# The second layer by sorted (token, expert) pairs in 44 steps, where every token ran all eight experts

## The chip, the cores and the metric

One core of a Trainium2 chip runs the whole kernel. The metric is the device time of one execution in microseconds, lower is better. Engines are named as the profile names them: PE (matrix multiply), DVE (vector), ACT (scalar), POOL (GpSimd), SP (issues transfers).

## What is computed

`x` is 2048 tokens of 512 numbers. Two layers follow each other, each with a layer norm ahead of it and a residual around it.

```python
x = x + xattn(layernorm(x), itok, ctx, ctx, ctx)
x = x + ffn(layernorm(x), G, gate_w, up_w, down_w, lora_A, lora_B)
# xattn, for a token whose id lies in quarter e of the vocabulary (4 of them):
#   h = x @ ctx[e].T ;  y = (silu(h) * h) @ ctx[e].T          512 x 512 both
# ffn: 8 experts, each 512 -> 64 (gate and up) -> 512, and LoRA 512 -> 16 -> 512
#   w = softmax(x @ G), all but the two highest set to 0
#   out = sum_e w_e * (down_e(silu(gate_e x) * up_e x) + lora_B_e(lora_A_e x))
```

Only two of the eight weights `w_e` of a token are not zero.

## The kernel before

**Layer one.** A prologue sorts the tokens by their quarter into 19 tiles of 128 tokens (`STEPS`), of which each has one matrix. Step k gathers tile k (POOL, `gather`), normalises it, transposes it on PE (`turn_x`, 4 blocks of 128x128), multiplies by the matrix (`l1_first`, 12 matmuls of 512 columns: each operand is split in a high part on ACT and a low part on DVE, and three of the four products of parts are taken), applies silu and the product on ACT and DVE, transposes again (`turn_act`), multiplies again (`l1_second`, 12 matmuls of 512 columns), adds the residual (DVE, `residual`), and POOL stores the rows to DRAM (`x1_rows`) at their compact places.

**Layer two.** It takes the 16 full tiles of 2048 rows in order. All eight experts are computed densely for each tile: `l2_first` makes 12 matmuls in each of three column groups (392, 384 and 384 columns: gate, up and LoRA of all experts and the 8 router logits), `l2_gates` makes the routing weights in twelve small DVE operations, `l2_act` multiplies them in, with zeros for the six experts not chosen, and `l2_second` makes 15 matmuls of 512 columns.

**Order.** Each engine executes its own list in program order. A semaphore wait holds up everything behind it on that engine. The order in a step is written by hand. In layer one PE does `turn_act(k-1)`, `l1_first(k)`, `turn_x(k+1)`, `l1_second(k-1)`, and DVE does `lo_act(k-1)`, `residual(k-2)`, `statistics(k+3)` with `normalise(k+2)` inside it, `l1_gate(k)`, `lo_x(k+1)`. A semaphore is waited for and the instruction after it is the one that the profile shows waiting. The layer-norm statistics of layer two's rows are made by the same `statistics` when the stored tile is read back by SP (L223).

## Time and profile before

| what | us |
|---|---|
| median of 3 runs | 333.06 |
| lowest and highest of them | 330.94, 333.4 |
| the profiled execution | 331.94 |
| its span, first to last instruction | 330.1 |
| layer one, from its third step's `turn_act` to layer two's first | 33.63 to 146.03 |
| layer two, to the last store's issue | 146.03 to 322.54 |
| PE busy | 304.6 |
| DVE, POOL, ACT busy | 212.8, 108.7, 82.9 |

The profiled execution's own time has 1.84 us outside of its span. Positions in the table are microseconds from the start of the span.

### The profile page before, as it was taken

To read this page: it belongs to the slowest core of one execution; us is meant where nothing else is said; L and a number is where in the kernel's file an instruction comes from. 1 tells how busy PE (TensorE), PEld (TensorE's weight loads), DVE (VectorE), ACT (ScalarE), POOL (GpSimd) and SP (SyncE) were. 2 spreads that over 40 slices of the span, in tenths; PEclk is the share of its full clock that TensorE was granted. 3 is DMA by queue.
4 is the path that set the end of the run, shared out by engine and by line. 5 is a ranking of instruction groups with operands and counts; after the bars stand their busy time and mean duration, and the time that the engine had idled before them with its cause. 6 is when DMAs were issued, how large, how long until landed. Compare 5 with 4: busy or idle time off the path is not lost.

```text
span 330.1 us, 5390 instructions
## 1 busy us (share of the span) xinstructions
PE 304.6 (92%) x1636; PEld 269.1 (82%) x1637; DVE 212.8 (64%) x603; ACT 82.9 (25%) x158; POOL 108.7 (33%) x118
## 2 busy tenths in 40 slices
PE   1649997999999999999999999999999999999990
PEld 1636885888888888889999999999999999999970
DVE  7879865674666576467865686658756776557520
ACT  3523213232332323231212211221212121212110
POOL 1779834566566445431120111101110111011111
PEclk9979999999999999999999999999999999999996
DMA  7462685122212323222210122011110000000000
GB/s 252 164 213 73 165 318 213 70 95 71 90 64 95 95 64 115 75 64 65 66 64 0 64 64 64 14 50 64 64 38 26 32 32 32 0 32 34 32 28 37
DMA packets 8074, 26.37 MB, mean 80 GB/s; under 512 B 1408, under 2 KB 1408, under 8 KB 7424
## 3 DMA queue, kind: packets, MB, share of 16 engines
q0 software_dynamic: 4320, 14.16, 12.5%
q1 hardware_dynamic: 3744, 12.08, 11.3%
q8 instruction: 5, 0.08, 0.1%
q14 instruction: 5, 0.04, 0.0%
HBM read 17.06 MB, written 9.18 MB: 79 GB/s over the span
## 4 chain that ended last, share of the span: by engine, by line
PE 81%; POOL 6%; DMA 6%; issue 2%; DVE 2%; ACT 0%; DVEq 0%; ACTq 0%; POOLq 0%
PE p_y L681 10%; PE p_y L686 10%; PE p_y L682 10%; PE p_h L681 7%; PE p_h L686 7%; PE p_h L682 7%; PE p_aT L676 5%; PE p_xT L670 4%; PE p_a L682 3%; PE p_a L681 3%; PE p_a L686 3%; PE p_b L682 3%; PE p_b L686 3%; PE p_b L681 3%; DMA xin<-x,gather_row 3%
## 5 line engine op out<-in xcount | busy, mean ns | idle before, releaser
L492 DVE TENSOR_TENSOR aT_lo<-p_aT,aT_hi 128x512 fp32r<-128x512 f32 (+1 forms) x35 | 26.3, 752 | 85.8 <-ACT aT_hi L320 83.1
L253 POOL DMA_INDIRECT out<-xout,out_row x16 | 16.6, 1035 | 134.8 <-DVE xout L500 133.1
L320 ACT ACTIVATE aT_hi<-p_aT 128x512 fp32r<-128x512 f32 (+1 forms) x35 | 22.7, 648 | 106.2 <-PE p_aT L676 100.1
L253 POOL DMA_INDIRECT x_rows<-xout,x_row x19 | 19.7, 1038 | 55.0 <-DVE xout L500 54.7
L681 PE MATMUL p_y<-ctx_hi,aT_hi 128*128 x76 | 31.4, 414 | 2.5 <-DVE xout L500 2.4
L681 PE MATMUL p_y<-w_hi,aT_hi 128*128 128x512 f32 x75 | 30.7, 410 | 0.0
L682 PE MATMUL p_y<-ctx_lo,aT_hi 128*128 x76 | 29.8, 392 | 0.0
L681 PE MATMUL p_h<-ctx_hi,xT_hi 128*128 x72 | 29.8, 413 | 0.0
L682 PE MATMUL p_y<-w_lo,aT_hi 128*128 128x512 f32 x75 | 29.4, 393 | 0.0
L682 PE MATMUL p_h<-ctx_lo,xT_hi 128*128 x72 | 28.3, 392 | 0.0
L247 POOL TENSOR_TENSOR rstd<-var_eps,neg_half 128x1 f32<-128x1 f32 x35 | 23.1, 659 | 13.0 <-DVE var_eps L475 12.9
L469 DVE BATCH_NORM_STATS2 bn<-xin 128x6 f32 (+1 forms) x35 | 24.0, 684 | 2.5 <-DMA xin<-x,gather_row 2.5
L670 PE MATMUL p_xT<-ident,xn 128*128 128x128 f32 x140 | 21.1, 273 | 3.6 <-DVE xn L483 3.6
L488 DVE TENSOR_TENSOR xT_lo<-p_xT,xT_hi 128x512 fp32r<-128x512 f32 x35 | 23.9, 684 | 0.7 <-PE p_a L686 0.6
L483 DVE TENSOR_SCALAR xn<-xin,mean_var,rstd 128x512 f32 (+1 forms) x35 | 21.5, 616 | 4.3 <-DVE bn L469 3.5
L316 ACT ACTIVATE xT_hi<-p_xT 128x512 fp32r<-128x512 f32 x35 | 20.9, 596 | 9.8 <-PE p_xT L670 9.8
L670 PEld LDWEIGHTS p_xT<-ident,xn 128*128 128x128 f32 x140 | 17.3, 141 | 7.1 <-issue 3.4
L500 DVE TENSOR_TENSOR xout<-p_y,xin 128x512 f32<-128x512 f32 x34 | 23.1, 681 | 0.0
L681 PE MATMUL p_a<-w_hi,xT_hi 128*128 128x392 f32 x64 | 23.1, 361 | 0.0
L676 PEld LDWEIGHTS p_aT<-ident,act 128*128 128x128 f32 x156 | 19.2, 141 | 4.5
L676 PE MATMUL p_aT<-ident,act 128*128 128x128 f32 x156 | 22.8, 273 | 0.0
L682 PE MATMUL p_a<-w_lo,xT_hi 128*128 128x392 f32 x64 | 21.9, 342 | 0.0
(145 smaller groups left out, 663.5 us busy)
## 6 DMA issues: line engine op xcount, KB each, us to landing
whole<-ctx_t SPq DMA_DIRECT2D x4, 1024.0 KB, 6.5
xin<-x_rows SPq DMA_DIRECT2D x16, 256.0 KB, 2.6
whole<-w_up SPq DMA_DIRECT2D x4, 580.0 KB, 5.1
whole<-w_down SPq DMA_DIRECT2D x1, 1280.0 KB, 8.0
xin<-x,gather_row POOLq DMA_INDIRECT x19, 3.4
x_rows<-xout,x_row POOLq DMA_INDIRECT x19, 3.1
out<-xout,out_row POOLq DMA_INDIRECT x16, 2.9
ids<-token_ids SPq DMA_DIRECT2D x1, 8.0 KB, 1.6
```

Source lines behind the costliest of these rows:

```text
L247: nc.gpsimd.tensor_tensor(rstd[:, r % 2:r % 2 + 1], var_eps[:, r % 2:r % 2 + 1], neg_half[:], ALU.pow).then_inc(rstd_ready, 1)
L253: nc.gpsimd.indirect_dma_start(out=to, out_offset=bass.IndirectOffsetOnAxis(ap=rows, axis=0), in_=xout[:, r % 2, :], in_offset=None).then_ ...
L320: nc.scalar.activation(aT_hi[:, 0:cols], p_aT[:, 0:cols], ACT.Copy).then_inc(ahi_ready, 1)
L469: nc.vector.bn_stats(bn6[:, parity, :], x_rows_of(r)).then_inc(bn6_ready, 1)
L488: nc.vector.tensor_tensor(xT_lo[:], p_xT[:], xT_hi[:].bitcast(F32), ALU.subtract).then_inc(xlo_ready, 1)
L492: nc.vector.tensor_tensor(aT_lo[:, 0:cols], p_aT[:, 0:cols], aT_hi[:, 0:cols].bitcast(F32), ALU.subtract).then_inc(alo_ready, 1)
L500: nc.vector.tensor_tensor(xout[:, parity, :], y[:], x_rows_of(r), ALU.add).then_inc(xout_ready, 1)
L670: last = nc.tensor.transpose(p_xT[:, blk(i)], xn[:, parity, blk(i)], ident[:])
L676: last = nc.tensor.transpose(p_aT[:, blk(i)], act[:, blk(i)], ident[:])
L681: nc.tensor.matmul(to, hi[:, blk(i)], w_hi(i), start=(i == 0), stop=False)
L682: nc.tensor.matmul(to, hi[:, blk(i)], w_lo(i), start=False, stop=False)
L686: last = nc.tensor.matmul(to, lo[:, blk(i)], w_hi(i), start=False, stop=(i == blocks - 1))
```

## The change

The prologue sorts once instead of twice. Layer one has the same 19 steps, but each step now also prepares layer two for its own tile, which stays in SBUF (`rec`, 8 tiles): `residual` is followed by a second `bn_stats`, `statistics2` ends the statistics, ACT subtracts the mean (`centre`), PE transposes the tile (`turn_x2`), ACT copies it (`copy_x2T`), PE multiplies it by the router matrix in fp32 (`route`, 4 matmuls of 8 columns), and DVE takes the two highest experts (`choose`). After each batch of four tiles `owners` and `places` on DVE and `rank` on PE work out the routing weights and the place of each (token, expert) pair, in a list sorted by expert. POOL scatters each tile's rows twice (`scatter`), to `rows_a` under the token's lower expert and to `rows_b` under the higher one.

Layer two has 44 steps (`PAIRS`), 22 for the lower experts and 22 for the higher ones (phases A and B). Step s loads 128 sorted rows of one expert (SP, `load_pair`, an address that is read from SBUF), transposes them (`tx`), multiplies by that expert's 144 columns (`up`: 12 accumulating matmuls of 144 columns), applies the gate (`gate_silu`, `gate_up`), transposes the 80 columns (`ta`), multiplies back (`down`, 3 matmuls of 512 columns), and adds (`pair_finish`). Phase A scatters its sums by rows to `sums_b`; phase B loads those (`load_sum`) and scatters to `out`. Iteration i of each engine's list holds parts of several steps (`pair_iteration`): PE does up(i), ta(i-1), down(i-2), tx(i+2).

The instructions are no longer in loops: they are all written out. The core of the diff:

```diff
+NB = E2 - 1
+CAP = TOKENS + P
+DUMMY = NB * CAP
+XROWS = DUMMY + P
+META = 4
+ROW = D + META
+REC = D + 2 * META
+RSTD, MEAN, GATE, DEST = range(META)
+NOWHERE = 1 << 20
+EARLY = 7
+PHASE = TILES + NB - 1
...
+            def load_pair(s):
+                if s >= ARING:
+                    sp.wait_ge(stored[(s - ARING) % ORING], 16 * ((s - ARING) // ORING + 1))
+                row = sp.value_load(pair_row[0:1, s:s + 1], min_val=0, max_val=DUMMY)
+                rows = rows_a if s < PHASE else rows_b
...
+            def load_sum(s):
+                n = s - PHASE
+                if n >= YRING:
+                    sp.wait_ge(pair_done, s - YRING + 1)
+                row = sp.value_load(pair_row[0:1, s:s + 1], min_val=0, max_val=DUMMY)
+                sp.dma_start(pair_sum[:, n % YRING, :], sums_b[bass.ds(row, P), :]).then_inc(sum_landed[n % YRING], 16)
...
+            for i in range(RRING):
+                sp.wait_ge(scattered_a[i], 16 * (BATCHES[EARLY_BATCH][1] // RRING))
+            for s in range(ARING):
+                load_pair(s)
+            sp.wait_ge(lists_ready, 2)
+            for e in range(NB):
+                fill_region(0, e)
...
+            for s in range(EARLY, PAIRS + 3):
+                if s == PHASE:
+                    for t in range(STEPS - RRING, STEPS):
...
+                    for i in range(ORING):
+                        sp.wait_ge(stored[i], 16 * ((PHASE - i + ORING - 1) // ORING))
+                if s - 3 >= PHASE:
+                    load_sum(s - 3)
+                if EARLY + 2 <= s < EARLY + 2 + NB:
...
+            def scatter(t, phase):
+                b = t // 4
+                pool.wait_ge(dest_ready, b + 1)
+                pool.wait_ge(stats_put, b + 1)
+                rows, cols, done = ((rows_a, slice(0, ROW), scattered_a), (rows_b, slice(META, REC), scattered_b))[phase]
                 nc.gpsimd.indirect_dma_start(
-                    out=to, out_offset=bass.IndirectOffsetOnAxis(ap=rows, axis=0), in_=xout[:, r % 2, :],
...
+            def store(s):
+                pool.wait_ge(pair_done, s + 1)
...
+            def centre(t):
+                sc.wait_ge(stats2_ready, t + 1)
+                nc.scalar.activation(record(t), record(t), ACT.Identity, bias=neg_mean2[:, t:t + 1]).then_inc(xc_ready, 1)
...
+            def pair_iteration(i):
+                if 0 <= i - 1 < PAIRS:
+                    ah2(i - 1)
+                if i < PAIRS:
+                    gate_silu(i)
+                if i + 2 < PAIRS:
+                    hi2(i + 2)
+                if i < PHASE:
+                    mean_back(i)
...
+            for k in range(STEPS):
+                if k >= 1:
+                    hi_act(k - 1)
+                if k >= 2:
+                    centre(k - 2)
...
+            def residual(t):
+                dve.wait_ge(y_ready, t + 1)
+                if t >= RRING:
+                    dve.wait_ge(scattered_a[t % RRING], 16 * (t // RRING))
+                    dve.wait_ge(scattered_b[t % RRING], 16 * (t // RRING))
+                nc.vector.tensor_tensor(record(t), p_y[:], xin[:, t % XRING, :], ALU.add).then_inc(x1_ready, 1)
+                dve.wait_ge(x1_ready, t + 1)
+                nc.vector.bn_stats(bn6_2[:, t % 2, :], record(t)).then_inc(bn6_2_ready, 1)
+            def statistics2(t):
+                dve.wait_ge(bn6_2_ready, t + 1)
+                nc.vector.bn_aggr(mean_var2[:, t, :], bn6_2[:, t % 2, :]).then_inc(mean2_ready, 1)
+                dve.wait_ge(mean2_ready, t + 1)
+                nc.vector.tensor_scalar(neg_mean2[:, t:t + 1], mean_var2[:, t, 0:1], -1.0, None, ALU.mult)
+                nc.vector.tensor_scalar(var_eps2[:, t:t + 1], mean_var2[:, t, 1:2], EPS, None,
...
+            def pair_finish(s):
+                if s >= ORING:
+                    dve.wait_ge(stored[s % ORING], 16 * (s // ORING))
+                dve.wait_ge(o_ready, s + 1)
+                if s < PHASE:
+                    dve.wait_ge(x1_back, s + 1)
+                    other = x1_pair[:, s % 2, :]
+                else:
+                    n = s - PHASE
+                    dve.wait_ge(sum_landed[n % YRING], 16 * (n // YRING + 1))
+                    other = pair_sum[:, n % YRING, :]
+                nc.vector.scalar_tensor_tensor(pair_out[:, s % ORING, :], p_o[s % 2][:], pair_meta(s, GATE), other,
+                                               ALU.mult, ALU.add).then_inc(pair_done, 1)
...
+            for k in range(STEPS):
+                if k >= 1:
+                    lo_act(k - 1)
+                if k >= 2:
+                    residual(k - 2)
+                if k + 3 < STEPS:
+                    statistics(k + 3, between=k + 2)
+                elif k + 2 < STEPS:
+                    normalise(k + 2)
+                if k >= 2:
+                    statistics2(k - 2)
+                if k >= 3:
+                    choose(k - 3)
+                    if (k - 3) % 4 == 3:
+                        owners((k - 3) // 4)
...
+            def turn_x2(t):
+                pe.wait_ge(xc_ready, t + 1)
+                if t >= 1:
+                    pe.wait_ge(x2T_out, t)
...
+            def route(t):
+                c = t % 2 * E2
+                pe.wait_ge(x2T_out, t + 1)
...
-            def l2_first(r):
-                pe.wait_ge(xhi_ready, r + 1)
-                for to, c0, c1, ready in ((p_a, 0, GATE_B0, part_a_ready), (p_b, GATE_B0, GATE_C0, part_b_ready),
-                                          (p_h, GATE_C0, UPW, part_c_ready)):
-                    w = up_part(c0, c1)
-                    hi_passes(to[:, 0:c1 - c0], xT_hi, KB, *w)
-                    pe.wait_ge(xlo_ready, r + 1)
-                    lo_passes(to[:, 0:c1 - c0], xT_lo, KB, w[0]).then_inc(ready, 1)
...
-            def l2_second(r, to=p_y, between=None):
-                if to is p_y:
-                    pe.wait_ge(xout_ready, r)
-                pe.wait_ge(ahi_ready, r + 1)
...
+            def tx(s):
+                pe.wait_ge(pair_landed[s % ARING], 16 * (s // ARING + 1))
...
+                rows = pair_x_of(s)
+                for i in range(KB):
+                    last = nc.tensor.transpose(p_x[s % 2][:, blk(i)], rows[:, blk(i)], ident[:])
+                last.then_inc(tx_ready, 1)
...
+            def up(s):
+                e = pair_matrices(s)
+                to = p_u[s % 2]
+                def w(i, part_of):
+                    return up_w[:, bass.ds(e + i * E2, 1), part_of, :].rearrange("p a f -> p (a f)")
...
+                else:
+                    pe.wait_ge(gated_ready, s - 1)
+                hi_passes(to[:, 0:UP], lambda i: xT_hi[:, s % 2, blk(i)], KB, lambda i: w(i, 0), lambda i: w(i, 1))
+                pe.wait_ge(lo2_ready, s + 1)
+                lo_passes(to[:, 0:UP], lambda i: xT_lo[:, s % 2, blk(i)], KB, lambda i: w(i, 0)).then_inc(u_ready, 1)
...
+            def down(s):
+                e = pair_matrices(s)
+                cols = slice(s % 2 * P, s % 2 * P + P)
+                w = [down_hi[0:DK, bass.ds(e, 1), :].rearrange("p a f -> p (a f)"),
+                     down_lo[0:DK, bass.ds(e, 1), :].rearrange("p a f -> p (a f)")]
...
+                nc.tensor.matmul(to, aT_hi[0:DK, cols], w[0], start=True, stop=False)
+                nc.tensor.matmul(to, aT_hi[0:DK, cols], w[1], start=False, stop=False)
+                pe.wait_ge(al2_ready, s + 1)
+                nc.tensor.matmul(to, aT_lo[0:DK, cols], w[0], start=False, stop=True).then_inc(o_ready, 1)
+            def pair_iteration(i):
+                if i < PAIRS:
+                    up(i)
+                if 0 <= i - 1 < PAIRS:
+                    ta(i - 1)
+                if 0 <= i - 2 < PAIRS:
+                    down(i - 2)
+                if i + 2 < PAIRS:
+                    tx(i + 2)
             pe.wait_ge(rows_ready, 1)
+            turn_x(0)
...
+            for k in range(STEPS):
+                if k >= 2:
+                    turn_act(k - 1)
+                l1_first(k, between=turn_x1 if k == 0 else (lambda: turn_act(0)) if k == 1 else None)
+                if 1 <= k < STEPS - 1:
+                    turn_x(k + 1)
+                if k >= 2:
+                    turn_x2(k - 2)
+                if k >= 6 and (k - 6) % 4 == 0:
+                    if (k - 6) // 4 == EARLY_BATCH:
+                        total(EARLY_BATCH)
+                    rank((k - 6) // 4)
+                if k >= 1:
                     l1_second(k - 1)
-            turn_act(STEPS - 1, KB)
-            pe.wait_ge(w2_lo_ready, -(-DOWN0 // PIECE))
-            l2_first(STEPS)
-            turn_x(STEPS + 1, (STEPS + 1) % 2)
...
```

What stands on PE in layer one between the first product and the second, ahead of the change (`p_h` is the first product's bank, `p_y` the second's):

```order
L686 MATMUL p_h<-ctx_hi,xT_lo 128x512 [waits xlo_ready]
L686 MATMUL p_h<-ctx_hi,xT_lo 128x512 x3
L670 MATMUL p_xT<-ident,xn 128x128 [waits xn_ready]
L670 MATMUL p_xT<-ident,xn 128x128 x3
L691 TENSOR_LOAD step_expert
L691 ISA x2
L681 ISA [waits ahi_ready,xout_ready]
L681 MATMUL p_y<-ctx_hi,aT_hi 128x512
```

and with it (`rec` is the tile after layer one, two steps back):

```order
L979 MATMUL p_h<-ctx_hi,xT_lo 128x512 [waits xlo_ready]
L979 MATMUL p_h<-ctx_hi,xT_lo 128x512 x3
L910 MATMUL p_xT<-ident,xn 128x128 [waits xn_ready]
L910 MATMUL p_xT<-ident,xn 128x128 x3
L924 MATMUL p_x2T<-ident,rec 128x128 [waits x2T_out,xc_ready]
L924 MATMUL p_x2T<-ident,rec 128x128 x3
L968 TENSOR_LOAD step_expert
L968 ISA x2
L974 ISA [waits ahi_ready,x1_ready]
L974 MATMUL p_y<-ctx_hi,aT_hi 128x512
```

The transposes of `rec` stand ahead of the second product and wait for `xc_ready`, which ACT's `centre` gives.

DVE in the same step, before, from `lo_act` on:

```order
L492 TENSOR_TENSOR aT_lo<-p_aT,aT_hi 128x512 [waits ahi_ready]
L500 TENSOR_TENSOR xout<-p_y,xin 128x512 [waits stored1,y_ready]
L469 BN_STATS bn<-xin 128x6 [waits x1_landed1]
L483 TENSOR_SCALAR xn<-xin,mean_var,rstd 128x512 [waits xT_ready,rstd_ready,bn6_ready]
L473 BN_AGGR mean_var<-bn 128x2
L475 TENSOR_SCALAR var_eps<-mean_var 128x1 [waits mean_ready]
L504 TENSOR_TENSOR act<-silu,p_h 128x512 [waits silu_ready]
L488 TENSOR_TENSOR xT_lo<-p_xT,xT_hi 128x512 [waits xhi_ready]
```

and with the change, behind the same `aT_lo` and the sum, which now is written to `rec`:

```order
L658 BN_STATS bn_2<-rec 128x6 [waits x1_ready]
L620 BN_STATS bn<-xin 128x6 [waits x_landed3]
L634 TENSOR_SCALAR xn<-xin,mean_var,rstd 128x512 [waits xT_ready,rstd_ready,bn6_ready]
L624 BN_AGGR mean_var<-bn 128x2
L626 TENSOR_SCALAR var_eps<-mean_var 128x1 [waits mean_ready]
L662 BN_AGGR mean_var<-bn_2 128x2 [waits bn6_2_ready]
L664 TENSOR_SCALAR neg_mean<-mean_var 128x1 [waits mean2_ready]
L665 TENSOR_SCALAR var_eps<-mean_var 128x1
L671 COPY logits<-p_rt 128x8 [waits logits_ready]
L673 MAX top<-logits 128x8 [waits logits_out]
L674 MAX_INDEX top_at<-top,logits 128x8 [waits route_step]
L649 TENSOR_TENSOR act<-act,p_h 128x512 [waits silu_ready,route_step]
```

Between the sum and the gate (`act<-`) now stand a second `BN_STATS`, three more small operations and the choice of experts (L671 to L674). ACT's `centre` waits for L665.

SP in layer two, before:

```order
L214 DMA whole<-w_down 128x2560
L223 DMA xin<-x_rows 128x512 [waits xout_ready,stored1,stored0] x2
L223 DMA xin<-x_rows 128x512 [waits xout_ready,x1_landed0,stored1,stored0]
L223 DMA xin<-x_rows 128x512 [waits xout_ready,x1_landed1,stored1,stored0]
L223 DMA xin<-x_rows 128x512 [waits xout_ready,x1_landed0,stored1,stored0]
```

and with the change, in phase B:

```order
L271 DMA pair_sum<-sums_b 128x512
L262 TENSOR_LOAD pair_row [waits stored1]
L262 ISA x2
L264 ISA
L264 DMA pair_x<-rows_b 128x516
L270 TENSOR_LOAD pair_row [waits pair_done]
L270 ISA x2
L271 ISA
L271 DMA pair_sum<-sums_b 128x512
```

Each load now waits for the store of six steps before, reads its address from SBUF and alternates with a load of sums.

## Rows read from the trace of the kernel before

**Rows 1.** The page: busy time of each engine, and the chain by engine
```profile
PE 304.6 (92%) x1636; PEld 269.1 (82%) x1637; DVE 212.8 (64%) x603; ACT 82.9 (25%) x158; POOL 108.7 (33%) x118
...
PE 81%; POOL 6%; DMA 6%; issue 2%; DVE 2%; ACT 0%; DVEq 0%; ACTq 0%; POOLq 0%
```

**Rows 2.** Timeline of PE, layer one: start, length (us), engine, line, tiles
```profile
33.63 0.60 PE L676 MATMUL p_aT<-ident,act 128*128 128x128 f32 x4
...
94.72 0.60 PE L676 MATMUL p_aT<-ident,act 128*128 128x128 f32 x4
...
97.93 0.60 PE L670 MATMUL p_xT<-ident,xn 128*128 128x128 f32 x4
98.28 0.48 PE L681 MATMUL p_y<-ctx_hi,aT_hi 128*128 x1
...
101.14 0.60 PE L676 MATMUL p_aT<-ident,act 128*128 128x128 f32 x4
...
146.03 0.60 PE L676 MATMUL p_aT<-ident,act 128*128 128x128 f32 x4
```

**Rows 3.** Timeline of ACT and of DVE in the same step
```profile
95.36 0.60 ACT L320 ACTIVATE aT_hi<-p_aT 128x512 fp32r<-128x512 f32 x1 [2.56 <-PE p_aT L676]
...
95.99 0.69 DVE L492 TENSOR_TENSOR aT_lo<-p_aT,aT_hi 128x512 fp32r<-128x512 f32 x1 [2.11 <-ACT aT_hi L320]
96.60 0.68 DVE L500 TENSOR_TENSOR xout<-p_y,xin 128x512 f32<-128x512 f32 x1
97.19 0.68 DVE L469 BATCH_NORM_STATS2 bn<-xin 128x6 f32 x1
97.92 0.55 DVE L483 TENSOR_SCALAR xn<-xin,mean_var,rstd 128x512 f32 x1
98.38 0.17 DVE L473 BATCH_NORM_AGGREGATE mean_var<-bn 128x2 f32<-128x6 f32 x1
```

**Rows 4.** Timeline of DVE: two small operations, the second waiting for the first
```profile
151.44 0.20 DVE L528 RECIPROCAL z_rest_inv<-z_rest 128x8 f32<-128x8 f32 x1
151.68 0.17 DVE L530 TENSOR_TENSOR z_exp<-z_silu,z_rest_inv 128x8 f32<-128x8 f32 x1
```

**Rows 5.** Timeline of PE, layer two: the act transposes that begin a row
```profile
156.00 0.71 PE L676 MATMUL p_aT<-ident,act 128*128 128x128 f32 x5
...
307.04 0.71 PE L676 MATMUL p_aT<-ident,act 128*128 128x128 f32 x5
```

**Rows 6.** Timeline of PE: short and wide matmuls
```profile
11.70 4.90 PE L662 MATMUL p_y<-below,ones 128*128 128x128 f32 x32
...
232.44 0.34 PE L681 MATMUL p_a<-w_hi,xT_hi 128*128 128x392 f32 x1
232.61 0.34 PE L682 MATMUL p_a<-w_lo,xT_hi 128*128 128x392 f32 x1
```

**Rows 7.** Timeline of PE at its slow and its full clock
```profile
19.85 0.63 PE L670 MATMUL p_xT<-ident,xn 128*128 128x128 f32 x4 [3.25 <-DVE xn L483]
...
22.39 0.63 PE L681 MATMUL p_a<-ctx_hi,xT_hi 128*128 x1
22.82 0.63 PE L682 MATMUL p_a<-ctx_lo,xT_hi 128*128 x1
...
52.66 0.49 PE L681 MATMUL p_y<-ctx_hi,aT_hi 128*128 x1 [2.40 <-DVE xout L500]
...
53.23 0.39 PE L681 MATMUL p_y<-ctx_hi,aT_hi 128*128 x1
```

**Rows 8.** Timeline of POOL in the step of Rows 2
```profile
97.56 1.03 POOL L253 DMA_INDIRECT x_rows<-xout,x_row  x1 [1.77 <-DVE xout L500]
```

**Rows 9.** The page: DMA issues, KB each, us from issue to landing
```profile
xin<-x_rows SPq DMA_DIRECT2D x16, 256.0 KB, 2.6
...
x_rows<-xout,x_row POOLq DMA_INDIRECT x19, 3.1
```

**Rows 10.** Timeline of POOL: the last store
```profile
322.54 0.96 POOL L253 DMA_INDIRECT out<-xout,out_row  x1 [1.77 <-DMA out<-xout,out_row]
```

More of the change, by code:

```diff
@@ L561, in _ @@
+            def pair_iteration(i):
+                if 0 <= i - 1 < PAIRS:
+                    al2(i - 1)
+                if i < PAIRS:
+                    gate_up(i)
+                if 0 <= i - 2 < PAIRS:
+                    pair_finish(i - 2)
+                if i + 2 < PAIRS:
+                    lo2(i + 2)
+            split_ctx(0, 0)
+            split_ctx(1, 0)
+            statistics(0)
+            statistics(1, between=0)
             split_ctx(1, 1)
             lo_x(0)
-            normalise(one(1), first_use=True)
+            normalise(1)
@@ L564, in _ @@
             split_ctx(2, 0)
[L565 removed]
+            statistics(2)
             split_ctx(2, 1)
[L568 to L591 removed]
@@ L628, in _ @@
[L628 to L641 removed]
+            constants()
@@ new lines, in _ @@
+            lo_act(STEPS - 1)
+            residual(STEPS - 2)
+            statistics2(STEPS - 2)
+            choose(STEPS - 3)
+            lo2(0)
+            lo2(1)
+            residual(STEPS - 1)
+            choose(STEPS - 2)
+            statistics2(STEPS - 1)
+            pair_iteration(0)
+            choose(STEPS - 1)
+            owners(len(BATCHES) - 1)
+            pair_iteration(1)
+            places(len(BATCHES) - 1)
+            pair_iteration(2)
+            whole_lists()
+            for i in range(3, PAIRS + 2):
+                pair_iteration(i)
@@ L773, in _ @@
[L773 to L784 removed]
+                turn_x(1)
@@ new lines, in _ @@
+            turn_act(STEPS - 1)
+            turn_x2(STEPS - 2)
+            l1_second(STEPS - 1)
+            route(STEPS - 2)
+            tx(0)
+            tx(1)
+            turn_x2(STEPS - 1)
+            pe.wait_ge(w2_lo_ready, PIECES)
+            pair_iteration(0)
+            route(STEPS - 1)
+            pair_iteration(1)
+            total(len(BATCHES) - 1)
+            rank(len(BATCHES) - 1)
+            pair_iteration(2)
+            for i in range(3, PAIRS + 2):
+                pair_iteration(i)
```

1086 lines of the change are left out of this document (611 added, 475 removed).

## Prediction

> **What bounds the kernel now.** The page first: PE is busy 92% of the span, DVE 64%, and the chain that ended last lies on PE for 81% [rows 1]. So read PE's steps. In layer one the transposes that begin a step start at 94.72 and again at 101.14, 6.42 us apart, with no idle time marked in between [rows 2]; from 33.63 to 146.03 there are 17 such steps. In layer two 14 rows of tiles take from 156.00 to 307.04, 10.79 us each [rows 5]. DVE and ACT have slack: the low part of a step's second operand follows PE's transposes by 1.27 us, while PE has the first product to make [rows 2, 3]. PE sets the pace of both layers, and the last store's issue comes at 322.54, 7.56 us before the span ends [rows 10].
>
> What the change removes is large. Layer two takes 322.54 - 146.03 = 176.5 us, for eight experts of which six get zeros. A step of pairs holds 12 x 144 + 3 x 512 = 3264 columns against 21600 of a row of tiles, so 44 steps have 144 thousand against 346 thousand. The question is what the waits between the engines make of that.
>
> **Layer one with the change.** I take t = 0 at the first `turn_act` transpose of a step and walk the order of each engine. High part on ACT at 0.64, `lo_act` on DVE at 1.27 (95.99 - 94.72), `residual` at 1.88 [rows 2, 3]. The new `bn_stats` of the result must wait for it: an operation of 512 that waits for the one before starts 0.73 behind it (97.19 to 97.92), one that doesn't 0.6 [rows 3]. So it starts at 2.61, the old `bn_stats` at 3.21, `normalise` at 3.94, `bn_aggr` at 4.40 (0.46, rows 3). Then come five small operations, three of them behind a wait at 0.24 each [rows 4], so `stats2_ready` is there at 5.25. ACT's `centre` takes 0.60 as other ACTs of 512 do [rows 3]: 5.85. PE has meanwhile made the first product and `turn_x`, which ends at 3.56 (98.28 - 94.72, rows 2), and now stands at `turn_x2`, whose wait for `centre` stands **ahead of the second product**. It goes on at 5.95, needs 0.35 (97.93 to 98.28), then the second product 2.86 (98.28 to 101.14) [rows 2]: 9.16. Then `route`, 4 fp32 matmuls. The row of 16 fp32 matmuls of 128 columns (32 passes, 4.90 us) gives 0.30 each [rows 6]; 8 columns may cost less, since the weight loads may set this, so 0.9 to 1.2 for four, and I take 1.2, that row. The next step begins at **10.35 us instead of 6.42**. PE has no way round this: `residual` of tile k-2 stands behind `lo_act(k-1)` on DVE, which waits for this step's transposes. The idle part is 5.95 - 3.56 = 2.4 us a step.
>
> Sixteen steps of 10.35 are 165.6. In the steps 6, 10 and 14 `rank` on PE waits some 0.8 more for `owners`. Step 18 has no statistics of a tile to come, but its `rank` waits for the sum over 16 tiles: I count the same small operations to 10.7. The first one-hots are ready earlier, as one sort is left, which gives back 1 us at the start. So `turn_act(18)` starts at 33.63 - 1 + 165.6 + 2.4 + 10.7 = **211.3**, where it was 146.03: +65. What hides beside it: two scatters a tile on POOL (1.03 each, rows 8), with its gather and split some 8 of 10.4 us; `places` on DVE (about 14 small operations, 3 us), which ends before the next `lo_act`; the weight splits on ACT.
>
> **Between the layers.** From 211.3 = A on. DVE has `places` and `early_list` (8 operations on one partition) ahead of `lo_act(18)`, until A+1.3. POOL has `inverse_deviation2(17)` ahead of the last early scatters, which needs `statistics2(17)`, A+3.9. It ends at A+4.5, four scatters at 1.03 follow, and the last lands 3.1 us after its issue at A+7.6 [rows 8, 9]: A+10.7. SP's loads follow: I allow 0.5 for reading the address, then 2.6 to landing [rows 9]: `tx(0)` at A+14. DVE has `lo2(0)` and `lo2(1)` ahead of `residual(18)`, so the last tile's `turn_x2` comes at A+20. Then `up(0)`, `route(18)`, `choose(18)`, `owners(4)`, `rank(4)`, `places(4)` and `whole_lists` follow one another on PE, ACT and DVE with three iterations between them (about 40 small operations, 9 us, the rest PE and ACT): A+42. SP then makes seven loads of a place and seven fills, 0.7 each, and load 7 waits for the last of them to land: A+53, and iteration 5 ends at **A+57**. After such idle stretches the clock costs something: after 3.25 us of idle and four transposes PE's matmuls stood 0.43 us apart (22.39 to 22.82), the lower level of the two (1.2 GHz), where twelve else take 2.86, 0.24 each [rows 7, 2]; some 3 us of this are in the 57.
>
> **The steps of pairs.** A term with no row is the start-to-start time p of a 144-column matmul of split operands. Below: columns alone, 0.17 us for 392 (232.44 to 232.61) [rows 6], 0.065 for 144. Above: fp32 at 128 columns, 0.30 [rows 6], 0.335 for 144. The rows nearest in width are this one and the transposes of 128, four of which take 0.35 to 0.44, 0.11 each [rows 2]; scaled to 144 they are 0.335 and 0.12, and I take the middle, **0.23**, since either could be the kin. PE's own work in an iteration is 12 x 0.23 + 0.11 + 3 x 0.23 + 0.44 = 4.0 us. The other bound is a ring of waits: load s waits until store s-6 has landed. From the start of iteration i: `up` 2.76, an allowance of 0.3 for the address, `ta` 0.11, `down` 0.69, `pair_finish` 0.1 + 0.68, POOL starts 0.28 after the result (96.60 + 0.68 to 97.56), lands 3.1, SP 0.5, load 2.6, `tx` 0.15 + 0.44 [rows 3, 8, 9]: 11.7 us, and this `tx` ends three iterations after it began, so T is at least 3.9. The two are alike; with what they don't share I take T = 4.2. DVE's four operations of a step (0.6, 0.6, and some 0.9 for the small ones) and POOL's 1.03 lie beside it. In phase B three transfers of 256 KB fall in 4.2 us, 190 GB/s, which may add 0.1 to 0.3 and is in the range.
>
> Iterations 6 to 41: 36 x 4.2 = 151. Between the phases `load_sum(22)` waits for the last store of phase A, and load 26 behind it: 7.3 us where 3.7 are there, +3.6. The end: iterations 42 and 43 to the end of `up`, 6.8, the chain through `ta`, `down` and `pair_finish` 3.4, and from the last issue to the end 7.6 as before [rows 10]: 17.8.
>
> **Sum:** 211.3 + 57 + 151 + 3.6 + 17.8 = 440.7 of span, and 1.84 outside of it: **443 us**, against 331.94 of the profiled execution, which lies 1.1 under the median of 333.06. Layer one and what follows it cost 65 + 57, layer two's 176.5 shrink only to 172.
>
> **Rivals.**
> (a) Short matmuls go by columns, p = 0.065. Then `up` takes 0.78, PE's work is 2.0, but the ring of waits still gives 9.76 / 3 = 3.3 us. 36 x 0.9 = 32 less, and 8 + 2 less between the layers and at the end: 401. The 392-column rows speak for it, the fp32 rows against. In the Trainium skill, "TensorE: Matmul & The Clock Gate", section "Back-to-back issue gap", the array takes one column a cycle and narrow matmuls in a stream come about 81 ns apart; the wide rows here agree with a column rule (0.24 us for 512, 0.17 for 392), and by it the time would be this rival's, an estimate; no row here shows it for split operands of 144.
> (b) They go like fp32, p = 0.335: PE's work is 5.3, T = 5.5, 36 x 1.3 = 47 more and 10 more around it: 500.
> (c) The clock falls in layer one too, since PE idles 2.4 us in every step. At 0.43 a matmul the second product takes 2.4 us more, 17 steps, 41: 484. Against it stands the row with 2.40 us of idle ahead of it: the matmul two places behind follows in 0.57 us (52.66 to 53.23), where two take 0.86 at the lower level [rows 7]. The Trainium skill's same page, section "Part 1: The HAM clock gate", has the clock fall after idle time and rise after steady work; both are seen here, at 19.85 to 22.82 [rows 7], but a gap repeated in every step isn't.
> (d) The other side: the round trips don't bind, since the engines run further ahead of one another than I read from their lists, and occupancy alone sets the time. Layer one is then 6.42 + 0.35 + 1.2 = 8.0 a step on PE, 33 + 17 x 8.0 = 169, some 10 between, 44 steps at DVE's 2.4, 106, and 15: 302. It turns faster than before when 110 of the 141 us that I count for waits and slow short matmuls are not there. Nothing in the order of the instructions allows it in layer one.
>
> **How the numbers follow.** The forecast (p from 0.12 to 0.28) has 0.52, 415 to 470; (a) 0.25, 385 to 415; (b) 0.08; (c) 0.08; (d) and other ways to be faster 0.05, equal 0.02. The range 385 to 485 holds the forecast, (a) and (c), 0.85. Under 1% can't be told from no change here: faster 0.05, same 0.02, slower 0.93.
>
> **What would show it.** In the profile after: 10.35 us between `turn_act` groups, with PE idle 2.4 us before the `rec` transposes, released by ACT's `rec`; the first `pair_x` transposes 14 us after the last `turn_act`; the start-to-start time of `up_w` matmuls; T of 4.2 and idle time before `pair_x` transposes released by a DMA. The prediction is wrong if `centre` is not what PE waits for, or if steps of pairs run under 3.3 us.

## The result and the profile after

The changed kernel took **496.12 us** (492.09 to 498.39, 4 runs) against 332.1 for the kernel before on the same chip: a ratio of 1.492, 95% interval 1.480 to 1.504. The direction was as forecast; the time lies 53 us above the forecast and 11 above its range. The profiled execution has a span of 490.3 us, 49.6 more than the predicted 440.7.

The page after, first what answers to [rows 1] (busy times of PE), then PE's busy tenths and the granted clock in tenths, in 40 slices of 12.3 us, then the chain by engine:
```profile
PE 388.8 (79%) x1799; PEld 328.9 (67%) x1799; DVE 237.3 (48%) x713; ACT 135.8 (28%) x301; POOL 155.7 (32%) x172
...
PE   2687777778788787886298099999897999799990
...
PEclk9999889899899989988655555555755555755555
...
PE 55%; DVE 13%; issue 11%; DMA 10%; ACT 5%; SPq 2%; POOL 2%; POOLq 0%; DVEq 0%
```
Read the two rows of digits together. In layer one PE is at 7 or 8 tenths and the clock near full. From the 21st slice on, in the steps of pairs, PE is busy nearly all the time but for some waits, **and the clock is at 5 tenths**, its lower level, in nearly every slice. The view by stretches says it sharper (us, busy time and count of PE, PEld, DVE, ACT and POOL, then PEclk, DMA share, GB/s):
```profile
160.00:215.00 55.00, 43.74 (x231) 34.85 (x228) 31.82 (x108) 18.51 (x39) 22.06 (x25) 0.97 0.16 57
215.00:270.00 55.00, 38.33 (x168) 33.03 (x168) 26.84 (x113) 13.51 (x36) 18.20 (x19) 0.64 0.27 93
...
300.00:350.00 50.00, 49.86 (x220) 44.72 (x219) 22.45 (x55) 18.23 (x44) 10.08 (x11) 0.54 0.46 154
...
353.00:417.00 64.00, 59.61 (x244) 52.57 (x242) 24.90 (x60) 14.71 (x39) 11.18 (x12) 0.50 0.40 118
```

**Layer one** goes as forecast. PE's timeline of a step, beside [rows 2]:
```profile
112.56 0.63 PE L916 MATMUL p_aT<-ident,act 128*128 128x128 f32 x4
...
115.83 0.60 PE L910 MATMUL p_xT<-ident,xn 128*128 128x128 f32 x4
118.49 0.65 PE L924 MATMUL p_x2T<-ident,rec 128*128 128x128 f32 x4 [2.06 <-ACT rec L442]
119.36 0.49 PE L974 MATMUL p_y<-ctx_hi,aT_hi 128*128 x1 [0.22 <-issue]
...
122.26 0.95 PE L936 MATMUL p_rt<-route_w,x2T 128*128 128x8 f32 x8
123.06 0.31 PE L916 MATMUL p_aT<-ident,act 128*128 128x128 f32 x1
```
10.50 us from `turn_act` to `turn_act` (10.35 forecast), PE idle 2.06 us ahead of the `rec` transposes and released by ACT's `centre` (2.4 forecast). The next step, in which `rank` stands between, takes 12.78; the fp16 matmuls of `rank` end, the queue idles again, and the second product falls to the lower clock at its second matmul, after which they start 0.40 to 0.43 us apart:
```profile
128.99 0.66 PE L924 MATMUL p_x2T<-ident,rec 128*128 128x128 f32 x4 [2.07 <-ACT rec L442]
...
130.60 0.50 PE L974 MATMUL p_y<-ctx_hi,aT_hi 128*128 x1 [0.73 <-issue]
130.93 0.60 PE L975 MATMUL p_y<-ctx_lo,aT_hi 128*128 x1
131.33 0.63 PE L974 MATMUL p_y<-ctx_hi,aT_hi 128*128 x1
131.75 0.63 PE L975 MATMUL p_y<-ctx_lo,aT_hi 128*128 x1
```

**The hand-over**, PE: the last `turn_act` of layer one (A), the first pair's transposes, the last tile's, and those of steps 6 and 7:
```profile
221.59 0.63 PE L916 MATMUL p_aT<-ident,act 128*128 128x128 f32 x4
...
237.03 1.11 PE L1015 MATMUL p_xT<-ident,pair_x 128*128 128x128 f32 x4 [4.83 <-DMA pair_x<-rows_a]
...
244.14 1.11 PE L924 MATMUL p_x2T<-ident,rec 128*128 128x128 f32 x4 [4.50 <-ACT rec L442]
...
280.87 1.11 PE L1015 MATMUL p_xT<-ident,pair_x 128*128 128x128 f32 x4 [12.83 <-DMA pair_x<-rows_a]
285.85 1.05 PE L1015 MATMUL p_a<-ident,pair_x 128*128 128x128 f32 x4
```

**A step of pairs** at the lower clock (4.81 to 5.3 us between `pair_x` transposes in most of them), and the place of one of the two rises to the full clock:
```profile
321.94 0.41 PE L974 MATMUL p_x2T<-up_w,xT_hi 128*128 x1
322.15 0.41 PE L975 MATMUL p_x2T<-up_w,xT_hi 128*128 x1
...
323.71 0.78 PE L1062 MATMUL p_y<-down_hi,aT_hi 80*128 x1
324.29 0.63 PE L1063 MATMUL p_y<-down_lo,aT_hi 80*128 x1
324.71 0.63 PE L1065 MATMUL p_y<-down_hi,aT_lo 80*128 x1
325.14 0.41 PE L1015 MATMUL p_a<-ident,pair_x 128*128 128x128 f32 x1
...
346.18 0.28 PE L975 MATMUL p_h<-up_w,xT_hi 128*128 x1
346.29 0.28 PE L974 MATMUL p_h<-up_w,xT_hi 128*128 x1
...
347.77 0.60 PE L1015 MATMUL p_xT<-ident,pair_x 128*128 128x128 f32 x4
...
352.47 0.33 PE L1015 MATMUL p_a<-ident,pair_x 128*128 128x128 f32 x1 [1.62 <-DMA pair_x<-rows_a]
```
The start-to-start time of a 144-column matmul is 0.21 us at the lower clock and 0.11 at the full one (read starts, not lengths: the lengths overlap). The clock rises inside the iteration from 344.51 to 347.77, which takes 3.26 us; in the next one, at the full clock, PE needs 3.08 us and then waits 1.62 for a load. From the transposes of step 7 to those of step 43 it is 179.3 us, 4.98 an iteration. The page's landings are what the forecast took from [rows 9]:
```profile
pair_x<-rows_a SPq DMA_DIRECT2D x22, 258.0 KB, 2.8
pair_x<-rows_b SPq DMA_DIRECT2D x22, 258.0 KB, 2.7
pair_sum<-sums_b SPq DMA_DIRECT2D x22, 256.0 KB, 3.1
```
The last store is issued late, as in [rows 10], but 10.9 us ahead of the end where it was 7.56:
```profile
479.43 0.97 POOL L364 DMA_INDIRECT out<-xin,pair_x  x1 [0.31 <-issue]
```

### The profile page after: what moved, and what is told of

It is laid out like the page before. It is cut to its first block, busy times and chain, and to the rows that moved or that the text cites. A ratio compares the mean times of both kernels' runs of the same rounds, so it can differ in the third digit from the quotient of the medians.

```text
span 490.3 us, 7034 instructions
## 1 busy us (share of the span) xinstructions
PE 388.8 (79%) x1799; PEld 328.9 (67%) x1799; DVE 237.3 (48%) x713; ACT 135.8 (28%) x301; POOL 155.7 (32%) x172
## 3 DMA queue, kind: packets, MB, share of 16 engines
q0 software_dynamic: 8080, 21.84, 12.3%
## 4 chain that ended last, share of the span: by engine, by line
PE 55%; DVE 13%; issue 11%; DMA 10%; ACT 5%; SPq 2%; POOL 2%; POOLq 0%; DVEq 0%
PE p_y L974 5%; PE p_y L975 4%; PE p_y L979 4%; PE p_xT L1015 3%; PE p_h L974 3%; PE p_h L975 3%; PE p_h L979 3%; PE p_a L1015 3%; PE p_x2T L975 3%; PE p_x2T L979 3%; PE p_rt L936 3%; PE p_x2T L974 3%; PE p_y L1062 3%; PE p_y L1063 3%; DMA out<-xin,pair_x 3%
## 5 line engine op out<-in xcount | busy, mean ns | idle before, releaser
L364 POOL DMA_INDIRECT sums_b<-xin,pair_x x22 | 21.4, 974 | 87.0 <-DVE xin L823 86.4
L364 POOL DMA_INDIRECT out<-xin,pair_x x22 | 21.4, 974 | 84.1 <-DVE xin L823 83.8
L809 DVE TENSOR_TENSOR aT_lo<-p_aT,aT_hi 80x128 fp32r<-80x128 f32 x44 | 12.7, 288 | 69.2 <-ACT aT_hi L485 68.5
L924 PE MATMUL p_x2T<-ident,rec 128*128 128x128 f32 x76 | 13.5, 304 | 39.9 <-ACT rec L442 39.2
L1015 PE MATMUL p_xT<-ident,pair_x 128*128 128x128 f32 x88 | 22.8, 411 | 22.6 <-DMA pair_x<-rows_a 17.7
L1015 PEld LDWEIGHTS p_xT<-ident,pair_x 128*128 128x128 f32 x88 | 17.1, 215 | 30.8 <-DMA pair_x<-rows_a 19.0
L974 PE MATMUL p_h<-up_w,xT_hi 128*128 x88 | 37.1, 423 | 0.0
L974 PE MATMUL p_x2T<-up_w,xT_hi 128*128 x88 | 36.4, 416 | 0.5 <-issue 0.5
L975 PE MATMUL p_h<-up_w,xT_hi 128*128 x88 | 35.7, 408 | 0.0
L975 PE MATMUL p_x2T<-up_w,xT_hi 128*128 x88 | 35.2, 403 | 0.0
L1062 PE MATMUL p_y<-down_hi,aT_hi 80*128 x44 | 32.8, 746 | 0.6 <-ACT aT_hi L485 0.4
L442 ACT ACTIVATE rec<-rec,neg_mean 128x512 f32<-128x512 f32 x19 | 13.7, 721 | 68.1 <-DVE var_eps L665 65.0
L974 PEld LDWEIGHTS p_h<-up_w,xT_hi 128*128 128x128 f32 x88 | 28.5, 324 | 1.5 <-issue 1.1
## 6 DMA issues: line engine op xcount, KB each, us to landing
sums_b<-fill SPq DMA_DIRECT2D x8, 256.0 KB, 10.9
```

Of the source, the lines that this page charges most:

```text
L364: nc.gpsimd.indirect_dma_start(out=to, out_offset=bass.IndirectOffsetOnAxis(ap=pair_meta(s, DEST).bitcast(U32), axis=0), in_=pair_out[:, s ...
L442: nc.scalar.activation(record(t), record(t), ACT.Identity, bias=neg_mean2[:, t:t + 1]).then_inc(xc_ready, 1)
L924: last = nc.tensor.transpose(p_x2T[:, blk(i)], rec[:, t % RRING, META + i * P:META + (i + 1) * P], ident[:])
L974: nc.tensor.matmul(to, hi(i), w_hi(i), start=(i == 0), stop=False)
L975: nc.tensor.matmul(to, hi(i), w_lo(i), start=False, stop=False)
L1015: last = nc.tensor.transpose(p_x[s % 2][:, blk(i)], rows[:, blk(i)], ident[:])
```

## The experiments

Two things were open: whether the low clock in the steps of pairs comes from the narrow matmuls or from the waits for loads, and what the order in layer one and the hand-over cost. "Theory A" in the expectations is that the narrow matmuls hold the clock down. "The mean iteration" is always the time from the transposes of step 7 to those of step 43, divided by 36; A is the last `turn_act` of layer one.

### e1_wide: twelve matmuls of 288 columns
```diff
-hi_passes(to[:, 0:UP], lambda i: xT_hi[:, s % 2, blk(i)], KB, lambda i: w(i, 0), lambda i: w(i, 1))
+hi_passes(to[:, 0:2 * UP], lambda i: xT_hi[:, s % 2, blk(i)], KB, both, both)
...
-lo_passes(to[:, 0:UP], lambda i: xT_lo[:, s % 2, blk(i)], KB, lambda i: w(i, 0))
+lo_passes(to[:, 0:2 * UP], lambda i: xT_lo[:, s % 2, blk(i)], KB, both)
```
`both(i)` is the high and the low part of a block's weights side by side, 288 columns.

> The same twelve matmuls of a step, each 288 columns wide in place of 144 (high and low part of the weights side by side; the second half of the columns is not read, and products are added that don't belong there, so the output is another). Theory A: PE's clock stays at its lower level in the steps of pairs because narrow matmuls leave the array idle between weight loads (0.213 us from one to the next at 0.50, where 144 columns need 0.12), though the profile has PE busy. Twice the columns then cost next to nothing and bring the clock back: 0.13 us each, an iteration of 2.8 us on PE, the ring of waits sets 3.4 to 3.9, and the time falls from 496 to some 450. Rival B: the clock is low because of the waits ahead, and the matmuls are simply slow: 0.24 us each, +0.3 us an iteration, some 510.

467.88 us (1.407, interval 1.398 to 1.415): **twice the columns, and 28 us less**, though not the 46 of theory A (some 450). The clock of the whole run is 0.88 against 0.73. PE's timeline:
```profile
320.92 1.11 PE L1015 MATMUL p_a<-ident,pair_x 128*128 128x128 f32 x4 [3.74 <-DMA pair_x<-rows_a]
...
322.78 0.44 PE L975 MATMUL p_h<-up_w,xT_hi 128*128 x1
323.02 0.44 PE L974 MATMUL p_h<-up_w,xT_hi 128*128 x1
323.26 0.44 PE L975 MATMUL p_h<-up_w,xT_hi 128*128 x1
```
Even at the lower clock 288 columns cost 0.24 us where 144 cost 0.21. Iterations run at 2.84 us until a load is late (here 3.74 us); the mean is 4.51. So the width matters for the clock, and behind it the ring of waits stands as the next bound, longer than the 3.4 to 3.9 us expected.

### e2_eight: four matmuls of 288 and four of 144
```diff
-hi_passes(to[:, 0:UP], lambda i: xT_hi[:, s % 2, blk(i)], KB, lambda i: w(i, 0), lambda i: w(i, 1))
+for i in range(KB):
+    nc.tensor.matmul(to[:, 0:2 * UP], xT_hi[:, s % 2, blk(i)], both(i), start=(i == 0), stop=False)
```


> Eight matmuls in place of twelve: four of 288 columns (high part of x by both parts of the weights) and four of 144. The sum of the cross product into the result is left out, so the output lacks it. Theory A: loads go from 12 to 8 and columns stay: at the lower clock 4 x 0.24 + 4 x 0.213 = 1.8 us in place of 2.56, 4.1 us an iteration, some 463; if the clock rises more often than before, less, down to 435. Rival B, columns set the time: 1728 columns as before, no change.

461.56 us (1.390, 1.382 to 1.399). A third fewer instructions bring 6 us over e1; the mean iteration is 4.43, with waits for loads in many. The instructions are hardly the bound; that the ring is, e6 shows.

### e3_order: the second product ahead of the `rec` transposes
```diff
-                if k >= 2:
-                    turn_x2(k - 2)
+                if k >= 3:
+                    route(k - 3)
+                if k >= 1:
+                    l1_second(k - 1)
...
-                if k >= 1:
-                    l1_second(k - 1)
                 if k >= 2:
-                    route(k - 2)
+                    turn_x2(k - 2)
```
(and ACT's `copy_x2T` goes last in its step)

> Only layer one: the transposes of the finished tile stand behind the second product, the router product one step later, so PE no longer waits for ACT's subtraction of the mean there. My theory: the 2.06 us of idle in each of 15 steps go, and with it the falls of the clock there: 496 to 460, steps of 8.2 to 8.5 us. Rival: DVE's own round (lo_act to gate and back, 7.5 us and some 5 us more in every fourth step) is next late and keeps steps at 9.5: 480.

447.17 us (1.345, 1.335 to 1.355): 49 less, 13 more than the theory gave. PE's timeline of a step:
```profile
118.41 0.65 PE L916 MATMUL p_aT<-ident,act 128*128 128x128 f32 x4 [0.62 <-DVE act L649]
...
122.49 0.96 PE L936 MATMUL p_rt<-route_w,x2T 128*128 128x8 f32 x8
123.30 0.48 PE L974 MATMUL p_y<-ctx_hi,aT_hi 128*128 x1
...
126.17 0.60 PE L924 MATMUL p_x2T<-ident,rec 128*128 128x128 f32 x4
126.60 0.60 PE L916 MATMUL p_aT<-ident,act 128*128 128x128 f32 x4
```
No idle time is left ahead of the `rec` transposes, and the granted clock is 1.00 from 27 to 175 us. Most steps take 7.6 to 8.5 us, the step after each `rank` 9.4 to 9.7 (DVE has `places` ahead of its `lo_act` there), and A comes at 175.85 instead of 221.59. Nearly all of the gain is there: from A to step 7 it is 64.8 us (64.3 in the changed kernel), the mean iteration 5.01. What cost time in layer one was the order of PE's own queue: a wait for `centre` with ready work behind it.

### e4_fill: other work on PE in every iteration
```diff
                 if 0 <= i - 2 < PAIRS:
                     down(i - 2)
+                if i == 4:
+                    pe.wait_ge(lists_ready, 2)
+                if i >= 4:
+                    for _ in range(4):
+                        nc.tensor.matmul(p_rt[:, 0:512], ones[:], wide_ones[:, 0:512], start=True, stop=True)
```


> The kernel as changed, and four f16 matmuls of 512 columns into an unused bank at the end of every iteration of the pairs from the fifth on (work that nothing needs). Theory A: they bring PE's clock to its full level: 2.5 + 0.85 us of PE an iteration, under the ring of waits, so 36 x 1.2 = 43 us less, some 450. Rival B, the clock is low because of waits and stays low: 4 x 0.43 = 1.7 us more in each of 41 iterations, some 560.

480.88 us (1.437, 1.422 to 1.452): with four more matmuls of 512 columns in each of some 40 iterations it is 15 us **faster**, where theory A gave 46 and rival B a loss of 64. The narrow matmuls are unchanged, so they can run at the full clock; iterations take 3.41 where nothing waits, but up to 7.2 where a load is late, 4.72 in the mean, and the granted clock from 285 to 455 us is 0.91.

### e5_ring: ten places for loaded rows, narrow matmuls
```diff
-ARING, YRING, ORING = 6, 4, 4
+ARING, YRING, ORING = 10, 4, 4
...
-            for s in range(ARING):
+            for s in range(min(ARING, EARLY)):
                 load_pair(s)
```
(places 6 to 9 lie in `pair_more`, in what `ctx_hi` leaves free after layer one)

> The ring of loaded rows gets 10 places in place of 6 (load s waits for store s-10), and the first seven loads all go ahead of the fills; the computation is whole. Theory A: what holds the clock at its lower level in the steps of pairs is that 144-column matmuls keep the array active too small a part of the time, though PE counts as busy; the ring of waits only matters where PE is fast. Then an iteration stays at 4.8 us, only the few odd stalls go (mean 4.98 to 4.85) and the first seven loads save 2 to 4 us: 482 to 491. Rival B: it is the waits of the ring that knock the clock down each time; without them it stays at the full level, an iteration takes 3.3 us, and 36 x 1.6 = 58 us go: 430 to 445.

475.08 us median, but 435.08 in one of four runs (the others 471.45 to 485.33), with a clock of 0.851 in that one and 0.71 to 0.74 in the others; no ratio can be given. In the profiled run the waits for loads inside the phases are gone, and most iterations take 4.81 us; the five ahead of the change of phase run at the full clock, 2.6 to 3.2 us each. The mean is 4.68. Three of the runs are near theory A's 482 to 491, the fourth is in rival B's 430 to 445. "Stays at 4.8" is too strong: without the waits the narrow form at times keeps a high clock once it has it, and neither this run nor another shows what starts that.

### e6_wide_ring: both


> The ring of 10 places together with first products of 288 columns (both halves of a split weight at once; the products of the low part with the low half are added where nothing reads them, and the cross product lies in columns that are not added to the rest, so the output differs). With 6 places the wide form took 467.9, mean iteration 4.54 with many waits for a load, 2.84 between them. Theory A: wide products can hold the full clock once nothing waits for a load: 2.9 to 3.1 an iteration, 36 x 1.5 = 54 us less than the wide form with 6 places: 405 to 420. Rival B: wide or narrow makes no difference and it ends with the narrow ring of 10, within 15 us of it. Rival C: the clock falls anyway from the gaps between the engines' chains: 445 to 465.

420.91 us (1.263, 1.251 to 1.276), a shade past the end of theory A's range, and the mean iteration is 3.17. PE's timeline, then a stretch as in the table above:
```profile
358.25 0.29 PE L980 MATMUL p_h<-up_w,xT_hi 128*128 x1
358.38 0.29 PE L979 MATMUL p_h<-up_w,xT_hi 128*128 x1
358.51 0.29 PE L980 MATMUL p_h<-up_w,xT_hi 128*128 x1
...
360.51 0.27 PE L1020 MATMUL p_xT<-ident,pair_x 128*128 128x128 f32 x1
```
```profile
350.00:400.00 50.00, 50.00 (x346) 46.01 (x345) 33.76 (x86) 18.31 (x51) 15.54 (x16) 0.99 0.82 259
```
PE is busy for 50.00 of 50 us here, as it is in the changed kernel, and the clock is 0.99. The four corners (us): narrow and 6 places 496.1, narrow and 10 475.1, wide and 6 467.9, wide and 10 420.9. The deeper ring is worth 21 with narrow matmuls and 47 with wide ones; the width 28 and 54. The 21 and the 54 rest on e5's median, whose runs lie between 435 and 485.

### e7_handover: the last tile ahead of the first pairs
```diff
-            tx(0)
-            tx(1)
             turn_x2(STEPS - 1)
-            pe.wait_ge(w2_lo_ready, PIECES)
-            pair_iteration(0)
             route(STEPS - 1)
-            pair_iteration(1)
             total(len(BATCHES) - 1)
             rank(len(BATCHES) - 1)
-            pair_iteration(2)
-            for i in range(3, PAIRS + 2):
+            tx(0)
+            tx(1)
+            pe.wait_ge(w2_lo_ready, PIECES)
+            for i in range(0, PAIRS + 2):
```
(DVE and ACT in the same manner)

> The last tile's residual, statistics, logits, choice, owners, rank, places and the whole lists are moved ahead of the first steps of pairs on PE, DVE and ACT; the ring stays at 6, the computation is whole. The chain from the last turn_act to the full list then no longer has three iterations in it: iteration 5 ends at A+45 to A+53 instead of A+65, so 476 to 484. If instead SP's scatters, fills and loads set the hand-over, less than 5 us go: 491 or more.

475.33 us (1.433, 1.419 to 1.446), 21 less: step 7's transposes come at A+47.4 instead of A+64.3. It also happens to settle the first question. Here no load was late inside phase A, and a stretch of its table reads:
```profile
270.00:350.00 80.00, 80.00 (x335) 73.16 (x334) 34.40 (x82) 28.22 (x66) 16.52 (x17) 0.50 0.44 144
```
PE busy 80 us of 80 without a gap, and the clock at 0.50 throughout. No wait holds it down here. What took it down was idle time before: it fell before 235 us, in the gap ahead of the steps of pairs, and stayed down until 415, over the whole phase A and the one wait of 3.80 us behind it.

### e8_all: order, hand-over, ring and the eight matmuls


> Four edits together: the order in layer one (second product ahead of the transposes of the result; alone it gave -49), the hand-over of the run beside this one, the ring of 10 places, and the first product as four matmuls of 288 and four of 144 columns (the cross product's sum is left out, so the output differs). Theory A: the terms add: -49, -15, and iterations of 2.9 to 3.1 in place of 4.98, -70: 350 to 375. Rival: the ring or the narrow four still drop the clock in the steps of pairs, then 400 to 430.

361.22 us (1.088, 1.078 to 1.098): the mean iteration is 3.06, A 177.84, step 7 at A+49.5, clock 0.92. The terms add to within 4 us: 49 (e3), 21 (e7) and 36 x (4.98 - 3.06) = 69 make 357 of 496. This form leaves out the sum of the cross product, as e2 does.

### e9_fill_ring: narrow matmuls, the other work, ten places


> The ring of 10 places, the first product as twelve narrow matmuls as in the changed kernel, and behind each iteration's down, from iteration 4 on, four f16 matmuls of 512 columns of ones whose result nobody reads; the output is the reference's. With the same added work and 6 places it took 480.9: iterations of 3.41 at full clock, 4.72 in the mean, broken by waits for loads. Theory A (the narrow matmuls keep the clock down, and where something else keeps it up the waits for loads bring it down again): with both gone the clock stays near 1.0 and an iteration takes 3.4: 36 x 1.57 = 57 us less than 496, and some 5 more at the hand-over, 430 to 440. Rival: the narrow matmuls themselves can't run at the full clock for long, whatever stands beside them: 460 to 480, with the clock under 0.7 in the steps of pairs.

445.73 us (1.335, 1.328 to 1.342), 6 us past theory A's range. Nearly every iteration takes 3.40 or 3.41; the mean of 3.83 holds the change of phase (9.4 us) and slow steps at the start of each phase. A stretch:
```profile
300.00:350.00 50.00, 50.00 (x355) 41.79 (x354) 28.59 (x73) 24.89 (x60) 14.57 (x15) 1.00 0.54 162
```
The rival falls: the same twelve narrow matmuls run at the full clock for 50 us on end with wide work beside them.

### e10_all_narrow: three edits, twelve narrow matmuls


> The order of layer one, the hand-over and the ring of 10 places together, with the first product as the changed kernel has it (twelve matmuls of 144); the computation is whole. If the three savings found alone add up (49, 21 and 21): 405, with iterations of 4.8 at the lower clock, 395 to 415. If the clock in the steps of pairs depends on how the layer before leaves it, then it stays high in part of them: 360 to 385. The difference to the run of four edits together (361) is what the four wide and four narrow matmuls are worth: 44 us by the first, under 20 by the second.

422.18, 423.12 and 433.64 us; the fourth execution stood at 1549.61, which nothing here explains, and no ratio is given. The first guess of 405 added the three savings (91) and is too low: 73 are there in the two fastest. The mean iteration is 4.59, with seven at 2.6 to 3.3 us ahead of the change of phase, as in e5. Against e8 the eight matmuls in place of twelve are worth 61 to 62 us. A stretch, with twelve narrow matmuls and nothing beside them:
```profile
285.00:307.00 22.00, 21.34 (x149) 18.69 (x149) 14.94 (x36) 11.16 (x29) 7.49 (x8) 1.00 0.23 76
```
So narrow matmuls alone do not bring the clock down either. It rose at 284 us, with PE busy throughout, and fell only at the change of phase, in a wait of 5.58 us for a load.

### e11_all_whole: the same with the halves added
```diff
+            def sum_halves(s):
+                dve.wait_ge(u_ready, s + 1)
+                nc.vector.tensor_reduce(u_sum[:, s % 2, :], p_u[s % 2][:, 0:2 * UP].rearrange("p (v f) -> p f v", v=2),
+                                        AX_X, ALU.add).then_inc(u_summed, 1)
```


> The four edits together, and the cross product's half added on VectorE (one operation that sums the two halves of 144 columns, some 0.45 us, and the gate on ScalarE reads the sum), so that the computation is whole. DVE has about 2.4 us of work in an iteration of 2.8: if the added operation is covered, 361 to 368; if DVE and the longer way from u to the gate bind, an iteration takes 3.2 to 3.4: 375 to 388. In either case slower than the kernel before, whose 332 would need another 30 us out of layer one and the hand-over.

373.69 us (1.119, 1.112 to 1.125), between the two forecasts. DVE's timeline has the added operation:
```profile
325.46 0.44 DVE L805 TENSOR_REDUCE u_sum<-p_h 128x144 f32<-128x288 f32 x1
```
Most iterations take 3.04 to 3.11 where most of e8's take 2.6 to 2.9, and the mean is 3.42 against 3.06, so it isn't covered. This is the fastest form found that computes all of it, and it is slower than the kernel before. Layer one ends at A = 177.50 (146.03, rows 2), and from there to the end of the span it is 194.7 us against 184.1 before (322.54 + 7.56 - 146.03, rows 2 and 10). With the clock at 0.88 and 1.00 in most of the steps (224.8 to 298.0 and 298.0 to 347.7 us) the sorted second layer still isn't shorter: the hand-over (21 us from A to `tx(0)`, 26 from there to `tx(7)`, at 0.77 and 0.73), the change of phase (10) and the end (24, at 0.60) eat what fewer columns save.

## Why the prediction was right in direction and short by 53 us

**Layer one: right.** The place (PE stands at the wait for `centre` ahead of a ready product) and the 10.35 us (10.50) hold, `route` is cheaper than forecast (0.8 us for four matmuls, not 0.9 to 1.2), and e3 shows the cause by removing it. Short by a little: the batch steps, 12.7 to 12.8 forecast as 11.15, since most of the second product runs at the lower clock. A is 221.59 instead of 211.3, **+10.3**: 4.7 in the three batch steps, 3.0 in two early ones (12.0 and 11.7), 1.4 in the last and 1.1 at the start. This is rival (c)'s mechanism, but only in these six of the 17 steps (granted clock 0.85 to 0.87); in the other eleven it is 1.00 over gaps of mostly 2.06 us. In e1, e2, e4 to e7 and e9, which have the same layer one, between five and ten steps take 11.5 us or more, so it isn't always the same steps.

**Between the layers: the chain right, sizes short.** `tx(0)` at A+15.4 (14), the last tile's transposes at A+22.5 (20), then the three iterations at the lower clock. Iteration 5 ends at A+65, not A+57: **+8**. e7 shows that the interleaved iterations and the order were worth 17 us of this.

**The steps of pairs: the step that failed.** "PE's own work in an iteration is 12 x 0.23 + 0.11 + 3 x 0.23 + 0.44 = 4.0 us." Here p was nearly right for the lower clock (0.21 for 0.23) and twice too high for the full one (0.11), and I took `down` and the transposes at the full clock beside it: 0.69 and 0.44, where they took 1.43 (323.71 to 325.14) and some 0.7 at the lower clock. At the lower clock the sum is 12 x 0.21 + 0.1 + 1.43 + 0.7 = 4.8, which is the period seen; at the full clock iterations of 2.6 to 3.3 us were seen (e5, e10).

I treated the clock as something that idle time lowers and work soon restores, as in layer one (down at 131 us, up again inside the microsecond from 134), and looked for idle time. The first half holds: in the traces of the changed kernel, e5, e7 and e10 each fall in the steps of pairs came with a wait for a load. The second doesn't hold for the narrow stream. In e1, with 288 columns, the clock was down at 321 us and up again by 328; in the changed kernel it stayed at 0.50 from 353 to 417, PE busy for 59.61 of 64 us, and rose there and at 346 with PE busy throughout. It was at the lower level with PE busy 80 us of 80 (e7), and at the full level with the same busy share when the matmuls were 288 wide (e6) or wide work stood beside them (e9). 36 iterations with the change of phase took 179.3 us instead of the forecast's 151 + 3.6 = 154.6: **+24.7**. Shown is that wide matmuls, or wide work beside narrow ones, bring the clock back after a fall (e1, e6, e9) where the narrow stream mostly stays down; why a stream that the profile counts as busy does not bring it back, no run shows.

The Trainium skill, "TensorE: Matmul & The Clock Gate", section "Part 1: The HAM clock gate", has the clock follow how busy the engine has been; by the profile's busy time the rows above contradict that, and only if "busy" means more than the profile counts do they agree. The Trainium skill, "Trainium Kernel Development and Optimization", section "Performance Expectations", warns that matmul busy time is a bad metric for how close a kernel is to roofline, because matmuls are pipelined; the trace agrees, since 144 columns take 88% of the time of 288 (0.21 to 0.24).

**The ring of waits: right, and hidden.** The bound of 3.9 us couldn't be seen at 4.81, but after each of the two rises of the clock PE soon waited for a load (1.62 us behind the iteration of 3.26, 1.89 behind that of 3.43), and e1 and e2 stood at 4.51 and 4.43, with iterations of 2.84 us between the waits in e1. The 3.9 was a floor. The ring cost 0.5 us more; that the gaps lower the clock again fits (e1 is at the lower level behind its wait of 3.74 us), but the 0.5 wasn't taken apart.

**The end:** 24.3 for 17.8, **+6.5**, the last iterations and the chain at the lower clock and 10.9 us after the last issue. The four terms make 49.5, the difference of the spans to 0.1. "176.5 shrink only to 172" compared unlike things: the 172 hold the 7.6 us behind the last issue, and with them layer two had 184.

**The rivals.** (a), p = 0.065 by columns, is out as a price at either level, though at the full clock 0.11 is nearer to it than to the 0.23 taken; the kin there was the transpose with its 0.11. (b), 0.335, is out too. (c) had the right resource mainly in the wrong layer; of its two rows only the fall stands at 19.85 to 22.82, the rise came at 24.1 us. (d) is out: even with four repairs it is 361, and 374 when whole. The range was too narrow above because it priced p and the clock apart, and let no case have the lower clock over the whole second layer.

## What to carry to other kernels

Before work is cut into narrow matmuls, price it at both levels of the clock: PE counted as busy is no sign that the clock is up, so read the row of the granted clock under the row of busy tenths, and ask of every wait whether the work behind it brings the clock back. Here one matmul with both halves of a split weight, or even useless wide work, was faster than the narrow stream. Look on every in-order queue for a wait that stands ahead of ready work (49 us here), and test a deeper ring only together with what makes the engine fast enough to need it (21 or 47 us).

## What the runs showed of the hardware that I had not expected

- Twelve 144-column matmuls of split operands start 0.21 us apart at the lower clock and 0.11 at the full one; 288 columns take 0.24 and 0.13. Twice the columns cost 14 to 18% more. That the weight loads set the floor fits, but no run shows it.
- PE busy 80.00 of 80 us with a clock of 0.50 (e7), and busy 50.00 of 50 with 0.99 and 1.00 (e6, e9). The narrow stream alone ran at 1.00 for 22 us (e10): it keeps the clock that it has, and mostly doesn't win it back after a fall.
- Adding four 512-column matmuls to each iteration shortened the kernel by 15 us with 6 places. With 10 it is 29 against e5's median, but e5's fastest run (435) is faster than e9's (444).
- With narrow matmuls and ten places the same program took 435 to 485 us, by how long the clock stayed up. What starts such a stretch stays open.
